# Normalised rows stored as two fp16 pieces and read back transposed, in a gated attention and expert kernel

## The reference

```
q  = layernorm(x)                                   # over the 512 columns
a  = gamma * softmax(q_h^T ctx_h / sqrt(16)) ctx_h  # 8 heads of 16 rows each
x1 = x + tanh(g_xattn) * a
u  = layernorm(x1)                                  # the normalised rows
h  = u @ down_w + down_b                            # 512 -> 256
l  = u @ router_w + router_b - cost                 # 8 logits; the two best experts
y  = sum over 2 experts of gate * (gelu(gelu(h) @ w1) @ w2) + 0.1 * shared expert
out = x1 + tanh(g_ffn) * (y @ up_w + up_b + gelu(u) @ core_w + core_b)
```

## Time and profile before

| | us |
|---|---|
| median of 3 runs (704.84 to 709.47) | 705.38 |
| profiled execution | 702.09 |
| its span | 699.5 |
| PE busy | 655.4 (94%) |
| ACT busy | 531.0 (76%) |
| DVE busy | 512.5 (73%) |
| POOL busy | 466.8 (67%) |

### The profile page before, as it was taken

The page is one execution under the profiler, slowest core; times in us unless marked ns, Lnnn a source line. Parts: engine busy times, 40 slices in busy tenths (PEclk is TensorE's granted clock), DMA queues, the critical chain, the costliest instruction groups (busy, mean ns, idle before and its releaser), DMA issues.

```text
span 699.5 us, 18429 instructions
## 1 busy us (share of the span) xinstructions
PE 655.4 (94%) x6005; PEld 344.4 (49%) x6005; DVE 512.5 (73%) x859; ACT 531.0 (76%) x1125; POOL 466.8 (67%) x468
## 2 busy tenths in 40 slices
PE   1799999999999999999999998879999999999998
PEld 0122222222222222222364554469889999998744
DVE  3989999999999999999779657554343343344466
ACT  2389999999999999999886747447677777777411
POOL 3698998988989888886658441405665665665722
PEclk9999999999999999999999999999999999999999
DMA  6655776666766666555254752459987997696596
GB/s 204 240 167 187 223 247 200 189 197 187 218 205 203 219 195 193 193 160 191 85 152 163 266 183 78 159 138 170 131 138 116 118 139 113 95 120 95 61 296 252
DMA packets 128482, 120.40 MB, mean 172 GB/s; under 512 B 64132, under 2 KB 97668, under 8 KB 128392
## 3 DMA queue, kind: packets, MB, share of 16 engines
q1 hardware_dynamic: 114968, 104.09, 51.7%
q0 software_dynamic: 12192, 14.16, 13.5%
q10 hardware_dynamic: 1232, 0.98, 0.5%
HBM read 60.25 MB, written 49.10 MB: 156 GB/s over the span
## 4 chain that ended last, share of the span: by engine, by line
PE 65%; POOL 13%; DMA 11%; ACT 3%; DVE 3%; issue 2%; SPq 1%; another core or an unknown queue 1%; POOLq 0%; DVEq 0%
PE EH L1333 24%; PE Y L1333 15%; PE pv L571 11%; PE ring L558 7%; PE nat L546 4%; ACT P L642 2%; DMA rd<-den_scratch 2%; DMA k_scratch<-khl 2%; POOL wlo L812 2%; DMA u<-in_wall 2%; DMA q_scratch<-qhl 1%; POOL tn L746 1%; POOL y_sums L2231 1%; POOL khl L804 1%; POOL whi L808 1%
## 5 line engine op out<-in xcount | busy, mean ns | idle before, releaser
L717 DVE TENSOR_REDUCE mx<-nat 128x2 f32<-128x1024 f32 x256 | 296.2, 1210 | 14.5 <-PE nat L546 14.3
L642 ACT ACTIVATE P<-ring 128x512 f32<-128x512 f32 x512 | 281.1, 601 | 16.2 <-PE ring L558 10.2
L2231 POOL DMA_INDIRECT y_sums<-ysb,to x74 | 123.2, 1665 | 92.5 <-DVE ysb L2165 73.6
L571 PE MATMUL pv<-P,VT 128*32 128x256 f32 x2048 | 157.9, 392 | 0.4
L546 PE MATMUL nat<-KS,QS 48*128 48x512 f16 x512 | 113.1, 395 | 21.1 <-DMA QS<-q_scratch 15.1
L558 PE MATMUL ring<-QS,KS 49*128 49x512 f16 x512 | 119.0, 391 | 8.0 <-ACT P L642 6.8
L1333 PE MATMUL EH<-XA,whi 128*128 128x256 f16 (+1 forms) x688 | 104.8, 258 | 0.0
L1333 PE MATMUL Y<-whi,u 128*128 x592 | 104.0, 273 | 0.1
L571 PEld LDWEIGHTS pv<-P,VT 128*32 128x32 f32 x2048 | 44.0, 108 | 99.3 <-issue 49.3
L2115 DVE TENSOR_TENSOR u<-X,u 128x512 f16<-128x512 f32 x62 | 42.6, 689 | 62.1 <-ACT u L1739 61.7
L1333 PE MATMUL EH<-XA,wlo 128*128 128x256 f16 (+1 forms) x344 | 84.7, 258 | 0.0
(11 more groups left out here) (282 smaller groups left out, 1029.3 us busy)
## 6 DMA issues: line engine op xcount, KB each, us to landing
QS<-q_scratch SPq DMA_DIRECT2D x64, 96.0 KB, 2.9
KS<-k_scratch SPq DMA_DIRECT2D x62, 96.0 KB, 2.3
u<-in_wall SPq DMA_DIRECT2D x7, 640.0 KB, 4.0
X<-in_x SPq DMA_DIRECT2D x16, 256.0 KB, 3.5
q_scratch<-qhl SPq DMA_DIRECT2D x16, 256.0 KB, 2.1
xr<-in_x SPq DMA_DIRECT2D x16, 256.0 KB, 3.4
rd<-den_scratch SPq DMA_DIRECT2D x16, 256.0 KB
u_rows<-un SPq DMA_DIRECT2D x16, 256.0 KB
```

The costliest lines, as they stand in the source:

```text
L571: m = pe.matmul(pv[32 * j:32 * j + 32, q], VT[i][:, lb, g, j, :], Pb[4 * (s % 2) + j][:, q], start=(lb == 0 and half == 0), stop=(lb == 3) ...
L642: act.activation(Pb[4 * (s % 2) + j][:, :], bank[:, :], ACT.Exp).then_inc(t_use.sem, 1)
L717: dve.tensor_reduce(mx[:, k // 8, :, k % 8], nat[k % 2][:, :, :], AX.X, ALU.max).then_inc(t_max.sem, 1)
L2231: pool.indirect_dma_start(out=ysum[:, :], out_offset=bass.IndirectOffsetOnAxis(ap=to[:, j % 2, a:a + 1], axis=0), in_=ysb[j % 2][:, a, :], ...
```

## The change

The second norm leaves POOL as two fp16 pieces (`uhi` the rounded values, `ulo` the remainder) that are stored together. `load_u` reads each piece of a group with one transposing DMA, of 512 by 512 elements, straight to where `h` reads it: `uh` and `ul` for odd groups, the buffer `XA` for even ones. PE's `uT`, ACT's two copies, DVE's `ul` and POOL's `uhp` go; DVE adds the pieces to `uf` in all groups. Group 3's load moves from ahead of the loop over groups to its second pass. In both norms POOL subtracts the mean itself (`xnegm` and `negm` go) and takes the score scale together with the epsilon under the root (`rs` goes). `un` no longer has a buffer of its own.

```diff
-    us = nc.dram_tensor("u_rows", [B, P, L], F32, kind="Internal").ap()
+    us = nc.dram_tensor("u_rows", [2, B, P, L], F16, kind="Internal").ap()
...
-            keys, queries = ("kh", "kl"), ("negm", "veps", "rstd", "rs", "qf", "qh", "ql")
+            keys, queries = ("kh", "kl"), ("veps", "rstd", "qf", "qh", "ql")
...
-            jobs += [(w - 3, n) for n in ("xnegm", "xveps", "xrstd", "u", "x1t")]
+            jobs += [(w - 3, n) for n in ("xveps", "xrstd", "u", "uhi", "ulo", "x1t")]
...
-                ck.wait(t_pool, s, "u")
-                sp.dma_start(us[s], un[:, :]).then_inc(t_us.sem, 16)
+                ck.wait(t_pool, s, "ulo")
+                sp.dma_start(us[:, s].rearrange("h p q -> p h q"), uhl[:, :, :]).then_inc(t_us.sem, 16)
...
-                ck.wait(t_pool, b - 1, "xveps")
+                ck.wait(t_pool, b - 1, "u")
...
             elif what == "u":
                 ck.wait(t_pool, b, "xrstd")
+                done(pool.tensor_scalar(un(b), ao[i][:, :], mvx[:, 0:1], lnx[:, 2:3], ALU.subtract, ALU.mult))
+            elif what == "uhi":
+                ck.wait(t_pool, b, "u")
                 ck.wait(t_us, b - 1)
-                done(pool.tensor_scalar(un[:, :], ao[i][:, :], lnx[:, 0:1], lnx[:, 2:3], ALU.add, ALU.mult))
+                done(pool.tensor_scalar(uhl[:, 0, :], un(b), 1.0, 1.0, ALU.mult, ALU.mult))
+            elif what == "ulo":
+                ck.wait(t_pool, b, "uhi")
+                done(pool.tensor_tensor(uhl[:, 1, :], un(b), uhl[:, 0, :], ALU.subtract))
...
-            elif what == "negm":
+            elif what == "veps":
                 ck.wait(t_dve, b, "aggr")
-                done(pool.tensor_scalar(v[:, 0:1], m[:, 0:1], -1.0, None, ALU.mult))
-            elif what == "veps":
-                done(pool.tensor_scalar(v[:, 1:2], m[:, 1:2], EPS, None, ALU.add))
+                done(pool.tensor_scalar(v[:, 1:2], m[:, 1:2], EPS, SCALE ** -2, ALU.add, ALU.mult))
...
-                done(pool.tensor_scalar(v[:, 3:4], v[:, 2:3], SCALE, None, ALU.mult))
-            elif what == "qf":
-                ck.wait(t_pool, b, "rs")
...
-                done(pool.tensor_scalar(qf[:, :], xt[i], v[:, 0:1], v[:, 3:4], ALU.add, ALU.mult))
+                done(pool.tensor_scalar(qf[:, :], xt[i], m[:, 0:1], v[:, 2:3], ALU.subtract, ALU.mult))
...
-        eng.wait_ge(t_pool.sem, t_pool.at[B + 1, "wlo"])
+        eng.wait_ge(t_pool.sem, max(t_pool.at[B + 1, "wlo"], t_pool.at[B - 4, "ulo"]))
...
+    even = flat(XA).bitcast(F16).rearrange("p (h k q) -> p h k q", h=2, k=LB)
+    high_of = lambda r: uh[:, :, :] if r % 2 else even[:, 0]
+    low_of = lambda r: ul[:, :, :] if r % 2 else even[:, 1]
...
-            ahead = cur([(n, k) for k in range(LB) for n in ("uT", "uh")]) + old([("a", 0), ("sah", 0)]) + cur([("lg", 0)]) + \
+            ahead = old([("a", 0), ("sah", 0)]) + cur([("lg", 0)]) + \
...
-            ahead = cur(four("ul")) + old([("sal", 0)]) + cur(R_(["lred", "lb", "lmx", "lsub", "lcl"] + route_a)) + low(0) + \
+            ahead = cur(four("uf")) + old([("sal", 0)]) + cur(R_(["lred", "lb", "lmx", "lsub", "lcl"] + route_a)) + low(0) + \
...
         def load_u(r):
             ends["stored"](sp, (r + 1) * G4 - 1)
-            if r in (1, 3):
-                wait(sp, t_pe, (0, 0, 0, 1)[r], "uT", LB - 1)
-            elif r == 2:
-                sp.wait_ge(t_z.sem, 4)
-            sp.dma_start(ub[r][:, :, :], us[r * G4:(r + 1) * G4].rearrange("t p q -> p t q")).then_inc(t_uu[r % 2].sem, 16)
+            if r == 1:
+                ends["stacks"](sp)
+            elif r >= 2:
+                wait(sp, t_pe, r - 2, "h", 1)
+                wait(sp, t_dve, r - 2, "uf", LB - 1)
+            for h, dst in enumerate((high_of(r), low_of(r))):
+                rows_ = us[h, r * G4:(r + 1) * G4].rearrange("t p q -> (t p) q")
+                sp.dma_start_transpose(dst, rows_).then_inc(t_uu[r % 2].sem, 16)
...
-            load_u(3)
...
                 if 1 <= r < NG - 2:
+                    load_u(3)
                     load_x(r + 1)
...
-            if name == "uT":
-                if i == 0:
-                    wait(pe, t_uu[r % 2], r)
-                for t in range(G4):
-                    m = pe.transpose(dst[:, t * P:t * P + P], ub[r][:, t, i * P:i * P + P], ident)
-            elif name == "lg":
+            if name == "lg":
                 for k in range(LB):
-                    wait(pe, t_act, r, "uT", k)
+                    wait(pe, t_dve, r, "uf", k)
...
-                    m = three(dst, slice(c0, c0 + P), uh[:, k, :], ul[:, k, :], k == 0, k == LB - 1)
+                    m = three(dst, slice(c0, c0 + P), high_of(r)[:, k, :], low_of(r)[:, k, :], k == 0, k == LB - 1)
...
-                wait(dve, t_pe, 0, "uT", i)
-                m = dve.tensor_copy(uf[:, i, :], bank(0, "uT", i))
+                if i == 0:
+                    wait(dve, t_uu[r % 2], r)
+                wait(dve, t_act, r - 1, "guh", i)
+                wait(dve, t_dve, r - 1, "gul", i)
+                m = dve.tensor_tensor(uf[:, i, :], high_of(r)[:, i, :], low_of(r)[:, i, :], ALU.add)
```

More of the change, by code:

```diff
@@ L57 @@
 R_MAX = K_QK
+UN_AT = 2 * NT * 16
 HALF = 64
@@ L832, in last_norm @@
         def last_norm():
-            for what in ("xnegm", "xveps", "xrstd", "u", "x1t"):
+            for what in ("xveps", "xrstd", "u", "uhi", "ulo", "x1t"):
                 job(Clock(pool), B - 1, what)
@@ L1037, in seq @@
         if engine == "pe":
-            ahead = cur(four("uT")) + older([("y", 1)]) + old([("a", 0), ("a", 1)]) + \
+            ahead = older([("y", 1)]) + old([("a", 0), ("a", 1)]) + \
                 cur([("lg", 0), ("lt", 0), ("h", 0), ("h", 1), ("rk", 0)] + ([("tot", 0)] if last else [])) + \
@@ L1075, in ffn @@
             t_xs.plan(r, n=G4)
-    early = {(0, "uT", k): k for k in range(LB)}
-    early |= {(0, "lg", 0): 0, (0, "lt", 0): 1, (0, "h", 0): 2, (0, "h", 1): 3}
+    early = {(0, "lg", 0): 0, (0, "lt", 0): 1, (0, "h", 0): 2, (0, "h", 1): 3}
     moved = {(t_act, (0, "lg", 0)): (t_dve, (0, "lpc", 0))}
@@ L1086, in ffn @@
         moved[t_dve, o] = t_pool, o
-    for k in range(LB):
-        moved[t_act, (0, "uT", k)] = t_dve, (0, "uf", k)
-        moved[t_act, (0, "uh", k)] = t_pool, (0, "uhp", k)
     ring = []
     for o in [o for r in BODIES for o in seq("pe", r) if o not in early]:
-        if o[1] in ("uT", "lg", "lt", "h", "a", "gt", "core", "rk", "tot"):
+        if o[1] in ("lg", "lt", "h", "a", "gt", "core", "rk", "tot"):
             ring.append(o)
@@ L1262, in rest @@
             wait(sp, t_dve, NG - 1, "r", "ro")
-            wait(sp, t_pe, NG - 1, "uT", LB - 1)
+            wait(sp, t_pe, NG - 2, "h", 1)
+            wait(sp, t_dve, NG - 2, "uf", LB - 1)
             def all_rows_out():
@@ L1527, in output @@
             m.then_inc(t_pe.sem, 1)
-        def rows_0(lo, hi):
-            if lo == 0:
-                ends["scores"](pe)
-            for k in range(lo, hi):
-                do(0, "uT", k)
         def logits_0():
+            ends["scores"](pe)
             pe.wait_ge(t_in.sem, t_in.value)
@@ L1601, in do @@
                 wait(act, t_pe, r, name, i)
-            if name == "uT":
-                wait(act, t_act, r - 1, "guh", i)
-                wait(act, t_dve, r - 1, "gul", i)
-                m = act.copy(uf[:, i, :], src)
-            elif name == "uh":
-                wait(act, t_pe, r - 1, "h", 1)
-                m = act.copy(uh[:, i, :], bank(r, "uT", i))
-            elif name == "lg":
+            if name == "lg":
                 wait(act, t_pe, r - 1, "lt", 0)
@@ L2189, in do @@
             m.then_inc(t_pool.sem, 1)
-        ops_0 = seq("pool", 0)
-        def some(*names):
-            def run():
-                for o in ops_0:
-                    if o[1:] in names or o[1] in names:
-                        if o == (0, "uhp", 0):
-                            ends["stacks"](pool)
-                        do(*o)
-            return run
         def output_bias():
@@ L2238, in rest @@
                 pool.tensor_tensor(*summands(n), ALU.add).then_inc(t_pool.sem, 1)
-        return {(2, "whi"): output_bias, (B - 3, "xnegm"): some(("uhp", 0), ("uhp", 1)),
-                (B - 2, "att"): some(("uhp", 2), ("uhp", 3))}, rest
+        return {(2, "whi"): output_bias}, rest
     return {"sync": sync, "tensor": tensor, "scalar": scalar, "vector": vector, "gpsimd": gpsimd}
```

53 lines of the change are left out of this document (19 added, 34 removed).

## The result

The changed kernel takes **744.8 us** (median of 4 runs, 742.7 to 745.2) against 705.1 us of the kernel before in the same session; the ratio is 1.055, 95% interval 1.050 to 1.060. The forecast was 707.0 with a range of 696.5 to 713.5; the result lies above it. The profiled execution of the change has a span of 743.2 us, 43.7 more than the 699.5 of before.

What follows compares the result with a forecast made beforehand. POOL was taken to set the pace in attention's first third and be cover afterwards, PE to be full in the groups. Attention +0.3, tables +0.3, group 1 +1.9 and +1.7, groups 2 and 3 -0.9 and -1.7: +1.6, 707.0 us, range 696.5 to 713.5.

Steps and rivals of the forecast that it cites:

- The merged operand forms of the remaining ones: POOL in attention: the norm operations that remain were given no added time for their merged operands.
- The cover: Attention: POOL's slack of 1.1 us per window; its cycle of 19.9 us still fits under DVE's 19.95.
- Copies and removals: POOL in attention: copy and subtraction to fp16 add 1.78 us, three removals save 0.69; net +1.0 us per window.
- The POOL rival: Attention: the write of `ao` waits for the store of x1, POOL becomes the pace; 713.5 us, chance 0.14.
- Last window and tables: Last attention window: work ready earlier against constant tables landing later; +0.3 us, between -1.6 and +1.8.
- The 1.6 us of earlier work: Last attention window: ACT's waits caused by PE's two portions of group 0 transposes go, gaining 1.6 us.
- The 1.8 us for a slower transfer: Load of group 1: transposing DMAs take 5.5 us and not 3.7, so the tables behind them land later.
- Group 1: After attention: `h` +1.9 us later because `uf` stands behind `gul` on DVE, and +1.7 for a fallen clock.
- Groups 2 and 3: After attention: `h` comes earlier, -0.9 us in group 2 and -1.7 in group 3.
- PE's time saved whole: Groups and last window: all PE time saved counts, given fast `uf` and timely tables; -11.1, 694.3 us, chance 0.17.
- The stall before 421.42 goes: Group 3: 3.6 us of PE's idle time and the clock loss behind it go; 703.4 us, chance 0.14.
- Slower transposing loads or a longer hold of SP: Loads after attention: at half the rows' rate the tables land 5 us later still; 711 us, chance 0.07.

Runs made afterwards that it cites:

- pieces alone: The changed kernel with the mean negated in its own operation again and added in both norms; 707.2 us beside 693.2, ratio 1.022.
- subtraction alone: The kernel before with the three small operations gone and the mean subtracted directly, rows stored and loaded as before; 700.3 us beside 693.2, ratio 1.010.
- one operation gone: The kernel before with the score scale taken under the root, the mean still negated and added; 704.6 us beside 703.6, ratio 1.002.

## Why the prediction was wrong

- **"The merged operand forms of the remaining ones I cost at nothing: same shapes." This is the step that failed.** In the two large ones it was not operands that were merged but an operator that was exchanged: addition for subtraction in two operations of 128x512 per window. The row that would have priced it on POOL was not in the trace of before (on DVE it was, at 0.55 us, and would have misled), and I gave it no bounds, though other unknown forms got theirs. Measured 2.08 against 0.76 us, +1.32 each, +2.64 per window. With that term in my own sum the cycle is 22.5 and attention +33; measured +32.1. The forecast had +0.3 for attention, and +6.5 at the upper end. Of the 42.1 us between the forecast of +1.6 and the measured +43.7 this step has 31.8.
- *The cover.* "It still fits, by 0.1 us" was right for what I had counted: with addition in place, DVE's statistics are 19.95 us apart. Three runs bear out that POOL has about 1.1 us of slack per window (pieces alone, subtraction alone, one operation gone).
- *Copies and removals.* 622, 1163 and 192 ns as taken. Net +1.0 holds.
- *The POOL rival* had the right engine and direction and the sign that it gave, a spacing of 20.3 us or more, was seen. Its mechanism, the write of `ao` waiting for the store of x1, wasn't the cause: POOL waited 0.8 us for it between 160 and 260. It had the wait of a store for its price and not the duration of an operation, so that the engine was right by another cause than the one given.
- *Last window and tables*, +0.3 with an upper end of 1.8. Measured +4.8 in the stretch. The issue that "grows with the size" was 5.7 us, near my outer value of 5.5; the wait of 3.98 us on DVE is what I had named, but I let PE's other products hide it. The 1.6 us of earlier work that I credited are there where POOL does not set the pace: from the last image's statistics to the last value product it is 59.5 us in the kernel before and 57.7 in the changed kernel with addition. With subtraction it is 64.4, so POOL's delay took them away. The 1.8 us for a slower transfer are not seen. The rule of the Trainium skill that I weighed, Advanced Engine Details and Errata, section X-Bar Transpose (TRN2), that transpose DMAs are as fast as regular ones, agrees with the traces as far as they show it: 5.1 to 5.5 us from issue to landing (medians by tile) against 4.8 to 6.2 for the plain loads of the same size. The short bursts of the expert loads were no measure. The time went into the hold on the issuing queue, as the run with plain loads shows.
- *Group 1*, +1.9 and +1.7 for the clock, 3.6 together. Measured +4.0. From the start of `gul` to `h` it is 8.1 us, against 7.8 in the forecast's sum: `gul` took 4.64 (4.00 before), `uf` 2.48, and the last `uf` ended 1.0 us before `h`, not 0.3. The other 1.7 us are that `gul` begins 5.5 us behind the first routed product and not 3.8. In between PE works at a granted clock of 0.50, from 399.2 to 406.0 us. So the clock did fall, but at the idle 3.44 us of group 0; behind the idle 3.24 us of group 1 it was granted in full. That the size fits is in part luck: no run separates the clock from the rest, and in the other trace of the same kernel the clock falls behind group 1's idle time as well, at 407.5 us.
- *Groups 2 and 3*, -0.9 and -1.7: measured +1.0 and +0.4. Four additions on DVE cost 2.5 us as estimated, but `h` comes 1.0 and 1.6 us behind the last of them and not 0.3, and in group 3 `guh` and `gul` are released 3.2 us behind the last core product, 2.5 before. The stall of the earlier trace rows is now passed on over `gul` and `uf`: PE is idle for 3.6 us before the logits of group 3, and the clock is at 0.64 behind it. Taking 16 transposes (1.92 us) off PE gave nothing.
- *The other rivals.* PE's time saved whole: excluded. The stall before 421.42 goes: it stayed. Slower transposing loads or a longer hold of SP (0.07, +4): the second half came true, for the stretch with the tables grew by 4.8 us, and issuing the tables first gave back 5.1 of the 5.5 us that the kernel with the negated mean loses there; the first half did not.

## What to carry to other kernels

When an instruction changes its operator and not its shape, it is a new form. If no row shows it on that engine, give it bounds like any unknown; the same form on another engine is no price (0.55 us on DVE, 2.08 on POOL). Here the nearest row on POOL was the two-input subtraction of the same size, 1.16 us. That alone would have added about 10 us to the forecast ((19.9 + 0.8 - 19.95) x 13), still far short of the result, but with the right sign. Two changes that share one engine's slack must be priced together; alone each may look nearly free. A large DMA issue is a cost of its queue before it is one of bandwidth, so look at what is queued behind it.

## What the runs showed of the hardware that was not expected

- On GpSimd, a per-partition scalar subtracted and multiplied over 128x512 fp32 takes 2.08 to 2.09 us in either order, subtracted alone 1.59, added and multiplied 0.76 to 0.77. With two full inputs the subtraction is not the slow one (1.16 us to fp16; an addition to fp32 takes 1.27 to 1.30). The Trainium skill, GPSIMD Engine Reference, section Engine selection, calls one-input element-wise work on GpSimd roughly line-rate, in a row on add, mul and max. The subtraction, 2.7 times as long as the addition over the same operands, can't be read so.
- Two transposing loads of 512 KB each hold SP's queue for 4.1 to 8.6 us (4.2 to 7.4 in the changed kernel), two plain ones for 0.9 to 1.5.
- A DVE addition or subtraction with two inputs of 128x512 took 0.68 us without a two-input operation of POOL beside it. With one it took longer in all traces, the `gul`, `uf` and `ul` of group 1's chain 1.75 to 2.19 us.
- The same instructions take 97 or 108 us between attention and the experts, depending on the chip or the session. In the slower case ACT and DVE (and PE, in the kernel before) stand for 2 to 3 us at one place, and the profile shows no releaser.
